# Four buffers for the context and mask rows, loaded and masked at other places of the loop

## The reference

```
x = x + L0_xattn(ctx, ctx, layernorm(x), ssm_kernel, D)   # causal convolution over the 256 positions
x = x + L0_ffn(layernorm(x))                              # gated, operands rounded to few bits
x = x + L1_xattn(layernorm(x), ctx, mask, mask)           # 16 heads of attention over 256 positions
x = x + L1_ffn(layernorm(x))                              # top 32 of 512 logits, softmax, two small products
```

```
q = Wq @ target + bq ; k = Wk @ source + bk ; v = Wv @ source + bv
dot  = mask * (q . k) / sqrt(8) - (1 - mask) * 1e6
out  = (softmax(dot) * mask) @ v
```

## Time and profile before

| what | value |
|---|---|
| median of 3 runs | 624.97 us (624.21 to 626.88) |
| span of the profiled execution | 623.6 us |
| DVE busy | 478.8 us, 77% of the span |
| PE busy | 491.8 us, 79% |
| ACT busy | 346.5 us, 56% |
| POOL busy | 400.9 us, 64% |
| mean granted TensorE clock | 0.918 of full speed |

### The profile page before, as it was taken

How to read it: one execution, slowest core, us unless ns; L and a number is a source line. 1 busy time by engine, 2 the same in 40 slices (tenths; PEclk the granted TensorE clock), 3 DMA queues, 4 the chain that set the end, 5 groups by cost and what they waited for, 6 DMA issues and landing times.

```text
span 623.6 us, 11640 instructions
## 1 busy us (share of the span) xinstructions
PE 491.8 (79%) x3633; PEld 280.0 (45%) x3633; DVE 478.8 (77%) x885; ACT 346.5 (56%) x578; POOL 400.9 (64%) x711
## 2 busy tenths in 40 slices
PE   1575888899796787979988988899987977887543
PEld 1464657666573343444444444444433433332221
DVE  4564658888889777899999999999978768784451
ACT  1246632313213475767877877778856657676431
POOL 6687487888897476677787787685654553422341
PEclk9888879999999798989999999999979879988875
DMA  6950100120235255544563465454464455411100
GB/s 195 371 114 7 29 17 2 26 44 0 75 42 125 52 97 127 115 82 110 95 122 102 86 142 109 78 140 96 95 145 98 86 130 104 87 29 39 46 8 17
DMA packets 92178, 54.31 MB, mean 87 GB/s; under 512 B 14851, under 2 KB 91844, under 8 KB 92118
## 3 DMA queue, kind: packets, MB, share of 16 engines
q1 hardware_dynamic: 92118, 53.58, 38.6%
HBM read 35.64 MB, written 17.42 MB: 85 GB/s over the span
## 4 chain that ended last, share of the span: by engine, by line
issue 20%; DVE 19%; PE 19%; DVEq 17%; POOL 15%; POOLq 7%; ACT 1%; ACTq 0%
PE pair L273 4%; PE bank L490 4%; POOL kv L888 4%; DVE w_int L1503 4%; DVEq L1544 3%; DVEq L1461 3%; DVEq L1554 3%; POOL yT L845 2%; DVEq L1412 2%; DVE prod L1365 2%; DVE best L1555 2%; DVEq L1515 2%; DVE st L1413 2%; DVEq L1440 2%; PE pair L461 2%
## 5 line engine op out<-in xcount | busy, mean ns | idle before, releaser
L1503 DVE TENSOR_REDUCE w_int<-pair 128x4 f32<-128x1024 f32 x128 | 155.6, 1216 | 23.0 <-PE pair L461 22.8
L1227 ACT ACTIVATE cT<-pair 128x1024 f32<-128x1024 f32 x128 | 130.9, 1023 | 62.1 <-PE pair L477 60.3
L273 PE MATMUL pair<-kv,toep 128*128 128x256 f32 x384 | 103.8, 411 | 27.9 <-POOL kv L888 10.6
L273 PEld LDWEIGHTS pair<-kv,toep 128*128 128x128 f32 x384 | 74.5, 205 | 48.3 <-issue 27.9
L888 POOL TENSOR_TENSOR kv<-cT 128x512 f32<-128x512 f32 x64 | 66.1, 1041 | 22.0 <-PE pair L273 15.9
L461 PE MATMUL pair<-KS,w_raw 54*128 54x256 bf16 x512 | 52.5, 285 | 30.0 <-DVE w_int L1503 29.9
L490 PE MATMUL bank<-cT,v_aug 128*32 128x256 f32 x1024 | 74.4, 411 | 0.0
L477 PE MATMUL pair<-w_raw,KS 57*128 57x256 bf16 x512 | 52.8, 287 | 15.8 <-DMA w_raw<-w_int 7.7
L1365 DVE TENSOR_TENSOR prod<-pair,qT 128x512 f32<-128x512 f32 x64 | 44.2, 691 | 24.8 <-PE pair L273 20.6
L461 PEld LDWEIGHTS pair<-KS,w_raw 54*128 54x128 bf16 x512 | 16.4, 97 | 73.2 <-DVE w_int L1503 58.7
L1372 DVE TENSOR_REDUCE yT<-prod 128x64 f32<-128x512 f32 x64 | 43.9, 686 | 6.2 <-issue 0.4
(11 more groups left out here) (163 smaller groups left out, 1013.6 us busy)
## 6 DMA issues: line engine op xcount, KB each, us to landing
w_raw<-scr_q SPq DMA_DIRECT2D x32, 192.0 KB
KS<-scr_k SPq DMA_DIRECT2D x32, 192.0 KB
scr_q<-w_int SPq DMA_DIRECT2D x16, 192.0 KB, 2.6
scr_k<-w_int SPq DMA_DIRECT2D x16, 192.0 KB, 2.6
scr_o<-qT SPq DMA_DIRECT2D x64, 36.0 KB
yT<-in_x SPq DMA_DIRECT2D x4, 512.0 KB, 7.5
ctx_all<-in_ctx SPq DMA_DIRECT2D x4, 512.0 KB, 7.9
x_b<-in_x SPq DMA_DIRECT2D x16, 128.0 KB, 5.2
```

The source lines that it names most:

```text
L273: mm = pe.matmul(bank[:, lh * n:(lh + 1) * n], toep[:, h, (lh - sh) * P:(lh - sh + 1) * P], rhs[:, sh, :], start=(sh == 0), stop=(sh == lh))
L1227: act.activation(probs[g % 4].rearrange("p j l -> p (j l)"), SC[:], ACT.Exp).then_inc(s("scores_free"), 1)
L1503: dve.tensor_reduce(neg_max[:, :, 2 * g:2 * g + 2].rearrange("p t j -> p j t"), M[:].rearrange("p (j t s) -> p j t s", t=KL, s=L), AX.X, A ...
```

## The change

The context and mask rows get four buffers each in place of two (`NC = 4`), and all index and wait arithmetic follows. The two loads are issued in another place of SP's loop: for sequence `m - 5` between `load_stacked_qk(m - 7)` and `load_x(m)`, where before they stood for sequence `m - 6` behind `load_max_rows`. The masking on POOL is called for sequence `m - 4` between `split_qk(m - 5)` and `add_attention(m - 9)`, where before it stood for `m - 5` behind `chosen_weights`. The projections stay where they are. No instruction is added or taken away.

```diff
+    NC = 4
...
-        ctx_m = [sb(f"ctx_m{k}", [P, L]) for k in range(2)]
-        mask_b = [sb(f"mask_b{k}", [P, L]) for k in range(2)]
+        ctx_m = [sb(f"ctx_m{k}", [P, L]) for k in range(NC)]
+        mask_b = [sb(f"mask_b{k}", [P, L]) for k in range(NC)]
...
             def load_context(b):
...
-                if b >= 2:
-                    sp.wait_ge(s("v_bank_ready"), b - 1)
-                    sp.wait_ge(s("x6_free"), turn6["qk", b - 2])
-                sp.dma_start(ctx_m[b % 2][:], a["ctx"][b]).then_inc(s(f"ctx{b % 2}_loaded"), 16)
+                k = b % NC
+                if b >= NC:
+                    sp.wait_ge(s("v_bank_ready"), b - NC + 1)
+                    sp.wait_ge(s("x6_free"), turn6["qk", b - NC])
+                sp.dma_start(ctx_m[k][:], a["ctx"][b]).then_inc(s(f"ctx{k}_loaded"), 16)
...
                 load_max_rows(m - 9)
-                load_context(m - 6)
                 load_denominator_masks(m - 7)
...
                 load_stacked_qk(m - 7)
+                load_context(m - 5)
                 load_x(m)
...
             def mask_context(b):
...
-                k = b % 2
-                pool.wait_ge(s(f"ctx{k}_loaded"), 32 * (b // 2 + 1))
+                k = b % NC
+                pool.wait_ge(s(f"ctx{k}_loaded"), 32 * (b // NC + 1))
...
                 chosen_weights(m - 11)
-                mask_context(m - 5)
                 later_products(m - 2, 3)
...
                 split_qk(m - 5)
+                mask_context(m - 4)
                 add_attention(m - 9)
```

More of the change, by code:

```diff
@@ L431, in project_qk @@
                 take6("qk", b)
-                pe.matmul(X6[:, L:2 * L], wqkvT[:, 1, :], ctx_m[b % 2][:], start=True, stop=True)
+                pe.matmul(X6[:, L:2 * L], wqkvT[:, 1, :], ctx_m[b % NC][:], start=True, stop=True)
                 pe.matmul(X6[:, 0:L], wqkvT[:, 0, :], xn2, start=True, stop=True).then_inc(s("qk_bank_ready"), 1)
@@ L444, in project_v @@
                     cols = slice(sh * P, (sh + 1) * P)
-                    pe.matmul(X7[:, cols], ctx_m[b % 2][:, cols], wqkvT[:, 2, :], start=True, stop=False)
-                    mm = pe.matmul(X7[:, cols], mask_b[b % 2][:, cols], bv0[:], start=False, stop=True)
+                    pe.matmul(X7[:, cols], ctx_m[b % NC][:, cols], wqkvT[:, 2, :], start=True, stop=False)
+                    mm = pe.matmul(X7[:, cols], mask_b[b % NC][:, cols], bv0[:], start=False, stop=True)
                 mm.then_inc(s("v_bank_ready"), 1)
@@ L692, in load_context @@
                     return
-                if b >= 2:
-                    sp.wait_ge(s("v_bank_ready"), b - 1)
-                    sp.wait_ge(s("x6_free"), turn6["qk", b - 2])
-                sp.dma_start(ctx_m[b % 2][:], a["ctx"][b]).then_inc(s(f"ctx{b % 2}_loaded"), 16)
-                sp.dma_start(mask_b[b % 2][:], bass.AP(a["mask"].tensor, b * L, [[0, P], [1, L]])).then_inc(
-                    s(f"ctx{b % 2}_loaded"), 16)
+                k = b % NC
[3 more added lines that the diff above has]
+                sp.dma_start(ctx_m[k][:], a["ctx"][b]).then_inc(s(f"ctx{k}_loaded"), 16)
+                sp.dma_start(mask_b[k][:], bass.AP(a["mask"].tensor, b * L, [[0, P], [1, L]])).then_inc(
+                    s(f"ctx{k}_loaded"), 16)
             def write_qk_parts(b):
```

## The result

The changed kernel took 710.0 us, the median of four runs (709.7 to 712.1), against 624.8 us for the kernel before on the same chip. The ratio is 1.136, with a 95% interval of 1.132 to 1.140: slower by 85 us. The span of the profiled execution went from 623.6 to 707.9 us, by 84.3.

What follows compares the result with a forecast made beforehand. DVE was taken to set the pace. Waits for x3 79, POOL's chain 11 and TensorE's clock 9, less 3 gained, gave 96 us over the 623.6 us span: 719.6, or 721 as median, range 680 to 750.

Steps and rivals of the forecast that it cites:

- DVE sets the pace in the middle: From 290 to 415 us DVE is busy 116.90 of 125 us, 24.77 us between readings of x3; waits before it add time.
- The load belongs to SP's next iteration: Context load, issued in SP's iteration m + 1 behind all eight stacked loads, makes x3 wait: 7.2 us, 11 times, 79 us.
- It lands late because of the queue: Context load behind the stacked operands on SP: landing 5.9 us after issue, like x_b, where its old place gave 2.1.
- The mask 1.3 us behind the context: Mask rows' landing after the context: 1.8 us undisturbed, partly covered by the backlog, so 1.3; mask lands at 354.4.
- The period grows to 32 us: Middle-stage iteration goes from 24.8 to about 32 us; loads restart from DVE's progress, so the loop cannot recover the wait.
- POOL's chain behind x3, 11 us: Slack behind x3 gone: 0.4 to 0.5 us at down_times_xr, PE about 0.5 late; 1.0 us in each of 11 iterations.
- The forecast's 0.5 us for PE: After normalise_x3, PE's next maxima product was to reach DVE about 0.5 us too late in each iteration.
- The clock, 9 us: PE idles most of 7 us per iteration; low clock on its work after x3 costs 0.8 us each, 9 in all.
- Only 3 of the 8.2 us gained: Of DVE's 8.2 us in five waits for PE's projection, only first and last count: 3 us gained, between 0 and 8.2.
- rival C: Loads in time at line 987: POOL's 19.0 and DVE's 8.2 us of waits vanish, nothing added; 617 us, chance 0.04.
- Rival A: Context lands as quickly in the new place as the old: 56 us more, 681 us; chance 0.16.
- Rival B: TensorE's clock falls in each longer wait, PE late each time, 26 instead of 9 us: 745 to 760 us; chance 0.12.

Runs made afterwards that it cites:

- early loads: The changed kernel with the context and mask loads of sequence m-5 issued at their old place behind load_max_rows, masking in its new place: 613.8 us, ratio 0.983 to the kernel before.

## Why the prediction was right

It said 721 us (680 to 750), slower, and 710 was measured. Step by step:

- **DVE sets the pace in the middle, so a wait in front of it is added to the time.** Right: 82.6 of 84.3 us are waits of DVE.
- **The load belongs to SP's next iteration and stands behind all that x3 needed.** Right, and the experiments tell the parts: neither place alone costs anything, the combination 96 us against 613.8.
- **It lands late because of the queue.** The context's landing was forecast at 5.9 us from the row of `x_b` and measured at 5.8. The formula of the Trainium skill's page "DMA: Bandwidth & Descriptors" (section on the anatomy of one DMA, 2.3 us by estimate) is fitted there to transfers that GpSimd issues, while here SP issues them, and it has no term for what stands in front; the 5.8 us measured here don't agree with it. What the same page says of the ring's order, under "Queues, rings and completion order", fits them. The context's own landing time of before, 2.1 us, came back as soon as the stacked loads stood behind it (median 2.2 us there).
- **The mask 1.3 us behind the context.** Too much: 0.5 us, almost the issue alone. Behind the backlog the mask's longer landing of before doesn't show. This term was mis-sized by 0.8 us an iteration, 9 us in all. The sum of the waits, 75.8 us for 79, hides it partly, since DVE now comes earlier to the reading: its waits before line 1493 are gone and have become part of the one for x3, as forecast. Both together were put at 79 - 3 = 76 us and measured at 76.2 - 7.9 = 68.3: 7.7 us of the miss of 11.7 (96 forecast, 84.3 measured in the spans).
- **The period grows to 32 us, and nothing gives it back.** 29 to 34.5 us.
- **POOL's chain behind x3, 11 us.** The mechanism is there, for 4.5 us at least and 10 at most. DVE came to line 1571 0.2 us later behind the reading of x3 than before in three of the nine iterations that have it, 0.5 us later in two and no later in four, where 0.4 to 0.5 had been put for each. At the full clock, in the run with 32 products, the whole chain costs 0.8 to 1.1 us in five iterations and nothing in three. The forecast's 0.5 us for PE doesn't follow from its own rows: the product that started at 354.92 ended at 355.31, 8.3 us behind x3, or 8.1 with the 0.2 us taken off; DVE needs it 7.1 us behind its reading, 7.2 behind x3. That makes it 0.8 to 0.9 us late.
- **The clock, 9 us.** Under-sized: 14.5 us of waits, 13 in the time. That the sum for both was near is partly luck, since one term was too high and the other too low: 20 us forecast, 23.1 measured against early loads over the eleven iterations. Against the kernel before DVE's waits for PE have grown by 14.3, 5.7 less than forecast. With the 7.7 us above that is 13.4; 1.7 us that stand in no marked wait go the other way and leave the 11.7.
- **Only 3 of the 8.2 us gained.** As a difference to before this can't be seen alone. But a version without the late load gains 11 us and not 8.2, since DVE's wait for PE's maxima products falls too, by 4.2 us, at a mean granted clock of 0.937 for 0.918. By the traces 3.9 us of it stand in the iterations of sequences 8 to 11, where before DVE waited 1.5 us at one product behind a low stretch of 3.4 or 6.8 us, and with early loads 0.5 to 0.7 us without one. That points at the clock; no run tests it. So rival C, 617 us, described a real possibility of this kernel that the two moves together missed.

Rival A failed on the landing times. Rival B had the mechanism right (by the trace's record of the clock, ten of the eleven low stretches at the waits were 10.2 us long, one 6.8) and the size wrong: only what DVE then waits for PE counts, mostly 1.2 to 2.4 us at its next maxima product, and a part of the low stretch falls into the wait itself.

## What to carry to other kernels

When a load and its first reader are both moved, write down for each the iteration in which it now happens, and compare the issue of the load with what the reader's engine did at that moment: here it was issued 0.7 to 2.5 us after POOL was ready for it, in every one of the eleven iterations. Take the landing time from a transfer of the same size in the same place of the queue, not from its own old place. And look at all that stands behind the reader on its in-order engine: with x3 out of the way the same wait cost nearly as much in the next two results.

## What I had not expected of the hardware

- A wait of PE of 6.1 to 8.7 us was followed by 6.8 to 10.2 us of the low level of its clock, half of the full one (a mean of 0.57 in the stretch from 354 to 362 us), which began while it waited. It cost 13 us here, and 32 products of no use in each wait, 6.8 us of them at the full clock, won it back; 22, which left 1.5 to 5.5 us of idling, won nothing (712.1 us).
- The mask rows, the same 1 KB read for all 128 partitions, took 1.2 to 1.4 us longer to land than the context where no stacked loads stood in front (3.3 to 3.5 against 2.1 us). Behind the backlog the two took the same, 5.9 and 5.8 us. Whether the repeated row makes the difference isn't shown: the mask was always issued right behind the context, 0.4 us later, so it never had the queue to itself.
